# Mixture of experts behind windowed and latent attention: expert tiles from tables, weights copied per tile, rests of the groups in slots of 64 rows

## The chip, the core and the metric

The kernel runs on one core of one Trainium2 chip. The metric is the device time of one execution in microseconds, median of several runs. Everything is float32 unless said otherwise.

## What is computed

The input x has 4 sequences of 512 tokens with 128 features, 2048 tokens in all. The first part is attention (16 heads in windows of 32 keys and the 32 before them, and 8 heads over 64 pooled latents per sequence, both gated), a projection, the residual sum and a layer norm. The second part sends each token through two of eight experts:

```python
h = jnp.mod(x_flat[:, :TOP_K].sum(axis=1).astype(jnp.int32), E)
sel = jnp.stack([h, jnp.mod(h + 1, E)], axis=1)
def step(acc, params):
    e, W1e, b1e, W2e, b2e = params
    w = jnp.any(sel == e, axis=1).astype(x.dtype) / TOP_K
    y = jnp.maximum(x_flat @ W1e + b1e, 0.0) @ W2e + b2e
    return (acc + w[:, None] * y, None)
```

Then come the residual sum and a second layer norm. W1 is 128x512 and W2 is 512x128 per expert. Tokens with the same h form a group; group g goes through experts g and g+1 (mod 8). With the inputs of the runs the eight groups have 1052, 324, 132, 35, 10, 29, 131 and 335 tokens; among the first three sequences they have 772, 249, 101, 27, 10, 26, 102 and 249.

## The kernel before, in words

Each of the five engines has its own program; they meet at semaphores. The attention part goes over 16 tiles of 128 tokens (T = 16), in a loop that is written out (lines 1337 to 1407 on TensorE, with its counterparts on the other engines). It is a software pipeline: in step t TensorE does the scores of tile t, the weighing of tile t-1 and the projection of tile t-3, so there are three steps more than tiles. In the last of them `keep_busy` (line 1279) issues matmuls on a constant, so that TensorE has work.

Behind the first layer norm VectorE finds each token's group (`mark`, line 889), its row in a table in DRAM, `seg`, that has a stretch of rows per group (`place`, line 894), and GpSimd scatters the rows there by indirect DMA (`scatter`, line 507). A row is 128 features and the token's index.

The expert part works on tiles of 128 rows of `seg`, all of one group. One tile is: a turn of the rows (`columns`, line 1294), four matmuls up with W1 of the first expert (into bank bA), four with W1 of the second (banks bB and bC), relus with bias into `ha` and `hb`, and eight matmuls down with W2, four per expert, all summed in one bank. VectorE then adds the bias and the row itself, takes mean and variance (`moments`, line 1029), GpSimd makes the reciprocal deviation (`deviation`, line 554), VectorE finishes (`finish`, line 1043), and GpSimd stores the rows by indirect DMA, one store waiting for the last (`store`, line 561).

There are two kinds of tiles:

- FULL = 5 tiles are written out (lines 1416 to 1440 on TensorE). They hold full tiles of groups among the first three sequences, so they can start while the last sequence is still in attention. Which they are is computed on VectorE (`full_tiles`, `full_rows`, lines 920 and 933), loaded into registers by each engine, and their W1 comes by DMA into `w1f`. Their bias is picked by VectorE (`full_biases`, line 946).
- All others come in eight loops, one per group (lines 1441 to 1460), whose bounds are loaded from a table (`count_tiles`, line 956). Inside a loop the expert is known when the kernel is built, so weights and biases have fixed addresses and only the tile number k is in a register. Each group has at least one tile in its loop, the last with rows of padding. The weights of all experts lie in SBUF (`w1_s`, `w2_s`).

In a loop tile ScalarE does the four relus of `ha` and two of `hb`, VectorE the other two (BA = 2), and VectorE copies the turned rows.

`load_table` (line 304) waits for a semaphore and loads entries into a sequencer's registers. In the trace such a load is TENSOR_LOAD, FUSED_REGOPS and SEQ_ASSERT on the engine's queue, all at line 306. A loop's end is ALU_OP and COMPARE_BRANCH. [...]

With these inputs there are 5 tiles written out and 4+3+2+1+1+1+2+3 = 17 in the loops.

Of the kernel before, what the change touches and what calls it, by code (L numbers as in the profile page):

```python
# [13 lines left out]
P = 128  # L14
# [4 lines left out]
def bass_windowed_latent_attention_hash_moe(  # L19
# [29 lines left out]
    SLOTS = T + E + 1  # L49

    with ExitStack() as ctx:
# [84 lines left out]
        tile_table = sb("tile_table", [1, 2, E + 1], I32)  # L136
        full = sb("full", [P, 3, Z + E + 1])
        taken = sb("taken", [P, E])
        jrow = sb("jrow", [P, 2, FULL])
        jint = sb("jint", [P, 2, FULL], I32)  # L140
        reached = sb("reached", [P, FULL, E])
        cover = sb("cover", [P, FULL, E])
        gone = sb("gone", [P, FULL])
        chosen = sb("chosen", [P, FULL, E])
        b1d = sb("b1d", [P, 2, FC, E])
        b1p = sb("b1p", [P, FULL, 2 * FC, E])
        b1x = sb("b1x", [P, FULL, 2 * FC])
        full_table = sb("full_table", [1, 2, FULL], I32)
        tile_scale = sb("tile_scale", [P, E])
        found = sb("found", [P, 2, FULL])  # L150


        w1_s = sb("w1_s", [P, E, F])
        w2_s = sb("w2_s", [P, E, FC, D])
        b1r = sb("b1r", [E * FC, P])
        b1c = sb("b1c", [P, E * FC])
# [3 lines left out]
        fsum = sb("fsum", [P, HEAD, D])  # L160
        w1f = sb("w1f", [P, WR, 2, F])
        xs = sb("xs", [P, D])
# [9 lines left out]
        idx = sb("idx", [P, 1], U32)  # L172

# [11 lines left out]
        bA, bB, bX, bY, bC = bS[0][:, 0:512], bS[0][:, 512:1024], bS[1][:, 0:512], bV, bT  # L185

# [49 lines left out]
        b1d_ok = sem("b1d_ok")  # L236
        b1x_ok = sem("b1x_ok")
# [69 lines left out]

        def expand(eng, dst, src, mask, n):

            return eng.tensor_tensor(  # L310
                dst, src.unsqueeze(1).to_broadcast([src.shape[0], n, src.shape[1]]),
                mask.unsqueeze(2).to_broadcast([src.shape[0], n, src.shape[1]]), ALU.mult)

        @block.sync
        def _(sp):
# [19 lines left out]
            for t in range(T):  # L335
# [6 lines left out]
                if t >= T - E - 4:  # L342
                    e = t - (T - E - 4)
                    if e < E:
                        sp.dma_start(w1_s[:, e, :], W1[e]).then_inc(f_in, 16)
                        sp.dma_start(w2_s[:, e, :, :], W2[e].rearrange("(c p) d -> p c d", p=P)).then_inc(f_in, 16)
# [9 lines left out]
            for j in range(FULL):  # L356
                rows += load_table(sp, full_table[:, 1, :], [j], full_ok, E * SEG - P)
                if j == 0:
                    experts += load_table(sp, full_table[:, 0, :], [j], full_ok, E - 1)
# [3 lines left out]
                if 1 <= j + 1 < WR:  # L363
                    experts += load_table(sp, full_table[:, 0, :], [j + 1], full_ok, E - 1)
                    load_full_weights(j + 1)
            for j in range(WR, FULL):
                experts += load_table(sp, full_table[:, 0, :], [j], full_ok, E - 1)
                load_full_weights(j)

            tail = load_table(sp, tail_table, [0], tails_ok, E * SEG - P)  # L370
            first = [FULL] + load_table(sp, tile_table[:, 0, :], [1], table_ok, T + E, FULL)
            sp.sem_inc(tile_in, 16 * FULL)
            sp.sem_inc(kept, 16 * FULL)
            sp.wait_ge(scattered_late, 16 * KT_)

            for e in range(E):
                if e > 0:
                    tail += load_table(sp, tail_table, [e], tails_ok, E * SEG - P)
                    first += load_table(sp, tile_table[:, 0, :], [e + 1], table_ok, T + E, FULL)
                with sp.Fori(first[e], first[e + 1]) as k:  # L380
                    i = nc.s_assert_within(k - first[e], 0, T - 1,
# [1106 lines left out]
```

## Time and profile before

| | |
|---|---|
| time, median of 3 runs | 239.04 us (238.46 to 239.31) |
| the profiled execution | 238.23 us, span 236.5 us |
| busy: TensorE, its weight load, VectorE, ScalarE, GpSimd | 90%, 75%, 62%, 51%, 50% of the span |
| mean clock granted to TensorE | 0.986 of full speed |
| moved by DMA | 14.73 MB, 62 GB/s |

The span is the time from the first to the last instruction of the profiled execution. A float32 matmul is two records in the trace, each with a weight load of its own. A busy share is a mean over stages with different limits, so the table says only where to look; the rows below are read for single stretches.

### The profile page before, as it was taken

How to read it: one execution, taken by the hardware profiler on the slowest of the kernel's cores; microseconds unless marked ns; L12 is line 12 of the kernel's file. 1: busy time of each engine (PE TensorE's matmuls, PEld its weight loads, DVE VectorE, ACT ScalarE, POOL GpSimd, SP SyncE). 2: the span in 40 equal slices, each digit the busy share in tenths (PEclk: the TensorE clock that was granted, in tenths of full speed). 3: DMA queues.
4: the chain of work that ended last, by engine and by line, in shares of the span. 5: the costliest groups of instructions: out<-in, count | busy, mean ns of one | idle time of the engine just before them, and what ended most of it. 6: DMA issues, size and time to landing. Idle time of an engine off the chain costs nothing.

```text
span 236.5 us, 10737 instructions
## 1 busy us (share of the span) xinstructions
PE 212.2 (90%) x4009; PEld 176.2 (75%) x4009; DVE 147.3 (62%) x521; ACT 120.6 (51%) x360; POOL 117.8 (50%) x219
## 2 busy tenths in 40 slices
PE   6879999999998999998999988999999999999920
PEld 2445778767777667886776678989999999899920
DVE  6836448585877765888898616734655555555540
ACT  3546557765466646765656145754344434344400
POOL 6563034852544427762647601847646545455541
PEclk9999999999999999999999999999999999999995
DMA  4131120112232132130001365212121212121100
GB/s 100 58 94 47 49 96 3 45 52 91 91 78 66 47 103 72 43 96 15 28 25 36 117 201 151 96 38 76 40 62 44 56 43 57 27 48 36 35 22 7
DMA packets 18557, 14.73 MB, mean 62 GB/s; under 512 B 2647, under 2 KB 15547, under 8 KB 18513
## 3 DMA queue, kind: packets, MB, share of 16 engines
q1 hardware_dynamic: 17008, 11.83, 17.9%
q0 software_dynamic: 1216, 2.16, 2.8%
q8 instruction: 30, 0.49, 0.9%
q10 hardware_dynamic: 288, 0.13, 0.3%
q14 instruction: 15, 0.11, 0.2%
HBM read 11.43 MB, written 3.03 MB: 61 GB/s over the span
## 4 chain that ended last, share of the span: by engine, by line
PE 74%; DVE 6%; issue 5%; DMA 4%; POOL 3%; ACT 3%; SPq 1%; POOLq 0%; ACTq 0%; DVEq 0%
PE bS L1308 12%; PE bT L1251 7%; PE bV L1452 6%; PE bV L1459 5%; PE bS L1194 4%; PE bV L1266 4%; PE bS L1219 4%; PE bJ L1170 3%; PE bV L1323 3%; PE bT L1308 3%; PE bS L1233 2%; PE bL L1367 2%; PE bS L1201 2%; PE bV L1274 2%; DMA out<-yo,idx 2%
## 5 line engine op out<-in xcount | busy, mean ns | idle before, releaser
L680 ACT ACTIVATE ha<-bS,b1c 128x128 f32<-128x128 f32 x68 | 19.4, 368 | 38.0 <-PE bS L1308 38.0
L668 ACT COPY PTs<-bT 128x512 f32<-128x512 f32 (+3 forms) x48 | 25.9, 539 | 18.2 <-PE bT L1251 18.2
L567 POOL DMA_INDIRECT out<-yo,idx x18 | 19.4, 1076 | 17.5 <-POOL idx L563 9.6
L1251 PE MATMUL bT<-ident,Pr 128*128 128x128 f32 x168 | 27.2, 277 | 0.5 <-issue 0.4
L1308 PE MATMUL bS<-xsT,w_s 128*128 128x128 f32 x204 | 26.3, 279 | 1.1 <-issue 1.0
L1308 PEld LDWEIGHTS bS<-xsT,w_s 128*128 128x128 f32 x204 | 24.1, 192 | 2.2 <-issue 2.2
L498 POOL TENSOR_SCALAR rstd<-mv 128x1 f32<-128x1 f32 x16 | 3.8, 236 | 44.0 <-DVE mv L859 44.0
L1251 PEld LDWEIGHTS bT<-ident,Pr 128*128 128x128 f32 x168 | 19.5, 141 | 5.4 <-issue 4.1
L514 POOL DMA_INDIRECT groups<-x,pos x16 | 16.5, 1034 | 11.7 <-DVE pos L909 8.4
L655 ACT ACTIVATE Pr<-bS 128x512 f32<-128x512 f32 x32 | 20.1, 629 | 3.0 <-PE bS L1233 3.0
L814 DVE TENSOR_REDUCE mx<-bS 128x8 bf16<-128x512 f32 x32 | 21.4, 677 | 0.0
L819 DVE TENSOR_REDUCE mx<-bS 128x8 bf16<-128x128 f32 (+3 forms) x16 | 7.9, 491 | 20.6 <-issue 14.9
L1459 PE MATMUL bV<-w_s,hb 128*128 128x128 f32 x136 | 18.5, 277 | 0.0
L1452 PE MATMUL bV<-w_s,ha 128*128 128x128 f32 x136 | 18.1, 276 | 0.2 <-DVE ysum L1027 0.2
L1077 DVE TENSOR_SCALAR hb<-bT,b1c 128x128 f32<-128x128 f32 x34 | 10.5, 347 | 11.7 <-PE bT L1308 11.0
L1459 PEld LDWEIGHTS bV<-w_s,hb 128*128 128x128 f32 x136 | 16.7, 191 | 0.3
L1452 PEld LDWEIGHTS bV<-w_s,ha 128*128 128x128 f32 x136 | 16.5, 192 | 0.4 <-ACT ha L680 0.4
L1266 PE MATMUL bV<-Vx,PTs 128*32 128x18 f32 x1024 | 15.2, 186 | 1.3 <-DVE rem L835 0.8
L1266 PEld LDWEIGHTS bV<-Vx,PTs 128*32 128x32 f32 x1024 | 12.4, 111 | 4.5 <-issue 3.2
L631 ACT COPY Vx<-bJ 64x256 f32<-64x256 f32 x32 | 12.0, 374 | 7.0 <-PE bJ L1170 6.8
L504 POOL TENSOR_SCALAR x<-y,mv,rstd 128x128 f32<-128x128 f32 x15 | 13.0, 867 | 1.6
L559 POOL TENSOR_TENSOR rstd<-rstd,half 128x1 f32<-128x1 f32 x22 | 12.5, 567 | 1.7
(237 smaller groups left out, 496.9 us busy)
## 6 DMA issues: line engine op xcount, KB each, us to landing
w_s<-in_L_ffn_W SPq DMA_DIRECT2D x16, 256.0 KB
w1f<-in_L_ffn_W SPq DMA_DIRECT2D x10, 256.0 KB, 3.0
xrow<-groups SPq DMA_DIRECT2D x22, 64.5 KB, 1.9
xs<-groups SPq DMA_DIRECT2D x18, 64.0 KB
x_tok<-in_L_attn_x SPq DMA_DIRECT2D x4, 256.0 KB, 3.7
groups<-padrows SPq DMA_DIRECT2D x1, 516.0 KB, 6.0
b2r<-in_L_ffn_b SPq DMA_DIRECT2D x1, 512.0 KB, 3.4
out<-yo,idx POOLq DMA_INDIRECT x18
```

Source lines behind the costliest of these rows:

```text
L504: nc.gpsimd.tensor_scalar(x1[:, t, 0:D], y[:, q, :], mv[:, q, 0:1], rstd[:, q, :], ALU.subtract, ALU.mult).then_inc(ln_done, 1)
L514: nc.gpsimd.indirect_dma_start(seg, bass.IndirectOffsetOnAxis(ap=pos[:, t:t + 1], axis=0), x1[:, t, :], None).then_inc(done, 16)
L567: nc.gpsimd.indirect_dma_start(rows_out, bass.IndirectOffsetOnAxis(ap=idx[:], axis=0), yo[:, FULL - 1, :], None, bounds_check=T * P - 1, o ...
L655: nc.scalar.activation(Pr[:, t % 2, j, :].rearrange("p (z c) -> p z c", z=2), own[j], ACT.Exp, scale=SCALE).then_inc(exped[j], 1)
L668: nc.scalar.copy(PTs[:, j, 0:m, :], bT[:, 0:m * P].rearrange("p (c q) -> p c q", c=m)).then_inc(turned_out, 1)
L680: nc.scalar.activation(dst[:, c, :], src[:, c * P:(c + 1) * P], ACT.Relu, bias=bias_of(c)).then_inc(relu, 1)
L814: nc.vector.tensor_reduce(mx[:, j, :].rearrange("p (z h) -> p z h", z=2), own[j].rearrange("p z (h k) -> p z h k", h=4), AX.X, ALU.max).th ...
L1251: last = nc.tensor.transpose(bT[:, c * P:(c + 1) * P], Pr[:, t % 2, j, c * P:(c + 1) * P], ident[:])
L1266: last = mm(bV[i * W:(i + 1) * W, a * PW:(a + 1) * PW], PTs[:, j, c, i * W:(i + 1) * W], Vx[:, q, i, a, :], start=True, stop=True)
L1308: last = mm(bank_of(c)[:, c * P:(c + 1) * P], w[:, c * P:(c + 1) * P], xsT[:], start=True, stop=True)
L1452: mm(bY[:, 0:D], ha[:, c, :], w2_s[:, e, c, :], start=(c == 0), stop=False)
L1459: last = mm(bY[:, 0:D], hb[:, c, :], w2_s[:, a, c, :], start=False, stop=(c == FC - 1))
```

## The change

- FULL is 4, one tile fewer written out. The later entries of the same table, up to the number of full tiles among the first three sequences, are run by a first loop on all engines. A second loop runs the remaining tiles from a second table. Table 1 has 12 entries of row and expert, table 2 has 14; both are computed on VectorE, on one partition.
- In both loops each engine but GpSimd loads one entry per tile (`load_entry`). The expert is now in a register. ScalarE copies the two experts' W1 (128x512 each) into the fixed tiles `w1a` and `w1b`; W2 and the biases are addressed through the register. The weights have a ninth entry, a copy of expert 0, so that e+1 needs no modulo.
- BA = 1: in a loop tile ScalarE does five relus and VectorE three. The loops sum in bank bL instead of bV.
- A group's rest of at most 64 rows (a longer one takes a full tile) goes to a slot. Eight slots of 64 rows make four tiles. Eight passes, one per expert in the order 1, 2, 3, 0, 4, 5, 6, 7, take the two slots that use this expert: four matmuls up with 128 moving columns, four relus on ScalarE, and four matmuls down where both slots lie in the same tile, otherwise four pairs of matmuls with 64 stationary columns each. The four slot tiles have buffers and stores of their own.
- In the last attention steps 18 fillers of `keep_busy` go and four come, and the first upward passes, which stood between the last steps' matmuls, come behind the last projection. `rank_last` stands ahead of an upward pass instead of behind it. `full_biases` goes.

With the inputs of the runs there are 4 tiles written out, 4 in the first loop, 8 in the second, and the four slot tiles.

```diff
-    BA = FC // 2
+    BA = 1
-    FULL = (EARLY * P - E * (P - 1) + P - 1) // P
+    FULL = (EARLY * P - E * (P - 1) + P - 1) // P - 1
+    TS = P // 2
+    TT = E // 2
+    ORDER = [1, 2, 3, 0, 4, 5, 6, 7]
...
+        def load_entry(eng, tab, i, most):
+            return eng.value_load(tab[0:1, bass.ds(i, 1)], min_val=0, max_val=most)
...
@@ scalar
+            act.wait_ge(down, FULL)
+            nc.scalar.copy(fsum[:, HEAD, :], bY[:, 0:D]).then_inc(f_out, 1)
+            act.wait_ge(f_in, 32 * (E + 1))
+            def tile_of(e, k):
+                act.wait_ge(up_a, k)
+                nc.scalar.copy(w1a[:], w1v[:, bass.ds(e * F, F)]).then_inc(w1a_ok, 1)
+                act.wait_ge(up_b, k)
+                nc.scalar.copy(w1b[:], w1v[:, bass.ds(e * F + F, F)]).then_inc(w1b_ok, 1)
+                act.wait_ge(up_a, k + 1)
+                for c in range(FC):
+                    nc.scalar.activation(ha[:, c, :], bA[:, c * P:(c + 1) * P], ACT.Relu,
+                                         bias=bias_of(e)(c)).then_inc(relu, 1)
+                act.wait_ge(up_b, k + 1)
+                for c in range(BA):
+                    nc.scalar.activation(hb[:, c, :], bB[:, c * P:(c + 1) * P], ACT.Relu,
+                                         bias=bias_of(e + 1)(c)).then_inc(relu, 1)
+            f1 = load_bound1(act)
+            with act.Fori(FULL, f1) as k:
+                tile_of(load_entry(act, experts1, k, E - 1), k)
+            f2 = load_bound2(act)
+            with act.Fori(f1, f2) as k:
+                tile_of(load_entry(act, experts2, entry_of(k, f1), E - 1), k)
...
@@ vector
-            first = [HEAD]
-            for e in range(E):
-                first += load_table(dve, tile_table[:, 1, :], [e + 1], table_ok, T + E, HEAD)
-                with dve.Fori(first[e], first[e + 1]) as last:
+            with dve.Fori(HEAD, last1) as last:
+                tile_of(load_entry(dve, experts1, last + 1, E - 1), last)
...
+                    nc.vector.tensor_scalar(hb[:, c, :], bC[:, c * P:(c + 1) * P],
+                                            b1c[:, bass.ds(e * FC + FC + c, 1)], 0.0, ALU.add, ALU.max).then_inc(relu_b, 1)
...
@@ tensor
-                if t == T + 2:
-                    keep_busy(6)
-                    columns(0)
-                    keep_busy(4)
-                    up_full(0, 0)
-                    pe.wait_ge(f_in, 32 * E)
-                    experts = load_table(pe, full_table[:, 0, :], [0, 1], full_ok, E - 1)
-                if t > T:
-                    keep_busy(6 if t == T + 1 else 2)
                 if t >= 3:
                     pe.wait_ge(gated, t - 2)
                     nc.tensor.transpose(aT, att[:], ident[:]).then_inc(attT_up, 1)
+                if t == T + 2:
+                    columns(0)
+                    pe.wait_ge(f_in, 32 * (E + 1))
+                    experts = load_table(pe, experts1, [0, 1], full_ok, E - 1)
...
-            for e in range(E):
-                a = (e + 1) % E
-                with pe.Fori(first[e], first[e + 1]) as k:
-                    up(lambda c: bA, k, w1_s[:, e, :], up_a)
-                    up(lambda c: bB if c < BA else bC, k, w1_s[:, a, :], up_b)
-                    pe.wait_ge(biased, k)
+            def tile_of(e, k):
+                pe.wait_ge(w1a_ok, k + 1)
+                up(lambda c: bA, k, w1a, up_a)
+                pe.wait_ge(w1b_ok, k + 1)
+                up(lambda c: bB if c < BA else bC, k, w1b, up_b)
+                pe.wait_ge(loop_biased, k)
+                for c in range(FC):
+                    pe.wait_ge(relu, by_act + c + 1)
+                    mm(bL[:, 0:D], ha[:, c, :], w2f[:, bass.ds(e * F + c * P, P)], start=(c == 0), stop=False)
...
+            with pe.Fori(FULL, f1) as k:
+                tile_of(load_entry(pe, experts1, k, E - 1), k)
+            f2 = load_bound2(pe)
+            with pe.Fori(f1, f2) as k:
+                tile_of(load_entry(pe, experts2, entry_of(k, f1), E - 1), k)
...
+            for i in range(E):
+                slot_pass_up(i)
+                if i + 2 < TT:
+                    tail_turn(i + 2)
+                if i >= 1:
+                    slot_pass_down(i - 1)
+            slot_pass_down(E - 1)
```

`slot_pass_down` issues, for an expert whose two slots lie in different tiles:

```python
for q, g in enumerate(groups):
    r = (g % 2) * TS
    last = mm(slot_sum[g // 2][r:r + TS, 0:D], h[:, c, q * TS:(q + 1) * TS], w2_s[:, e, c, :],
              start=opens[q], stop=False, skip_group_check=True)
```

## Rows read from the trace of the kernel before

**Rows 1.** The page: busy us, share of the span, count.

```profile
PE 212.2 (90%) x4009; PEld 176.2 (75%) x4009; DVE 147.3 (62%) x521; ACT 120.6 (51%) x360; POOL 117.8 (50%) x219
```

**Rows 2.** Stretches: length, busy us (count) by engine, clock, DMA share, GB/s.

```profile
159.50:226.40 66.90, 65.46 (x563) 63.54 (x562) 37.98 (x137) 28.14 (x102) 37.05 (x72) 1.00 0.19 48
226.40:236.50 10.10, 0.00 (x0) 0.00 (x0) 1.48 (x5) 0.00 (x0) 3.15 (x5) 0.68 0.03 11
```

**Rows 3.** Chain in order of time, loops: start us, us, what.

```profile
206.74 0.40 issue
...
211.08 1.34 PE bS L1308 x12
212.42 0.45 PE bT L1308 x4
212.86 0.89 PE bV L1452 x8
213.76 0.11 PE bS L1303
...
214.76 0.26 issue
215.02 1.60 PE bS L1308 x12
```

**Rows 4.** Line 306, the table loads: ns min/median/max, first and last start.

```profile
L306 PEldq FUSED_REGOPS  x13: 151/151/165, 137.9 to 214.5; - x13
L306 PEldq SEQ_ASSERT  x13: 18/18/18, 138.2 to 214.8; - x13
...
L306 PEldq TENSOR_LOAD <-tile_table x8: 296/300/307, 151.1 to 214.2; - x8
...
L306 DVEq TENSOR_LOAD <-tile_table x8: 300/304/314, 161.1 to 216.2; - x8
```

**Rows 5.** Line 1445, the loop's branch on TensorE's sequencer.

```profile
L1445 PEldq COMPARE_BRANCH  x17: 67/208/251, 162.8 to 225.6; - x17
```

**Rows 6.** Timeline of VectorE in one loop tile.

```profile
212.99 0.61 DVE L1077 TENSOR_SCALAR hb<-bT,b1c 128x128 f32<-128x128 f32 x2 [0.47 <-PE bT L1308]
...
214.87 0.29 DVE L1027 TENSOR_TENSOR ysum<-bV,b2s 128x128 f32<-128x128 f32 x1 [0.42 <-PE bV L1459]
...
216.03 0.18 DVE L1037 BATCH_NORM_AGGREGATE mv<-st 128x2 f32<-128x6 f32 x1
```

**Rows 7.** Timeline of TensorE, 138 to 160 us.

```profile
138.91 0.39 PE L1281 MATMUL bJ<-spare 128*128 128x256 bf16 x2 [0.62 <-issue]
...
145.11 0.19 PE L1288 MATMUL bJ<-onehot,before 128*128 128x32 bf16 x1 [0.90 <-DVE onehot L885]
...
159.53 0.72 PE L1308 MATMUL bS<-xsT,w_s 128*128 128x128 f32 x5
```

**Rows 8.** Groups by form: busy us, mean ns, idle before.

```profile
L668 ACT COPY PTs<-bT 128x512 f32<-128x512 f32 x36 | 21.2, 590 | 18.0 <-PE bT L1251 18.0
...
L680 ACT ACTIVATE ha<-bS,b1c 128x128 f32<-128x128 f32 x68 | 19.4, 368 | 38.0 <-PE bS L1308 38.0
```

**Rows 9.** Timeline of VectorE, first and last of 13 table operations.

```profile
146.81 0.15 DVE L958 TENSOR_SCALAR tiles<-nextrow 1x8 f32<-1x8 f32 x1
...
149.28 0.26 DVE L970 CAST tile_table<-tiles 1x9 int32<-1x9 f32 x1
```

**Rows 10.** Chain in order of time, the last two stores.

```profile
226.91 2.31 DMA out<-yo,idx
...
230.59 1.05 POOL out L567
```

**Rows 11.** Timeline of TensorE, weighing with 32 stationary columns.

```profile
130.64 0.71 PE L1274 MATMUL bV<-GVx,PTs 128*32 128x72 f32 x32
```

**Rows 12.** Stretches of TensorE's clock; columns as in rows 2.

```profile
134.00:136.00 2.00, 1.46 (x12) 0.92 (x10) 0.51 (x3) 0.27 (x1) 1.61 (x3) 1.00 0.70 243
...
230.00:236.50 6.50, 0.00 (x0) 0.00 (x0) 0.00 (x0) 0.00 (x0) 1.05 (x1) 0.50 0.02 6
```

More of the change, by code:

```diff
@@ L390, in _, with load_tile @@
-            sp.wait_ge(xT_up, first[E])
+            def load_tile(k, row):
+                sp.wait_ge(kept, k * 16)
+                sp.wait_ge(xT_up, k)
+                sp.dma_start(xs[:], seg[bass.ds(row, P), 0:D]).then_inc(tile_in, 16)
+                sp.dma_start(xrow[:, bass.ds(k * XW, XW)], seg[bass.ds(row, P), :]).then_inc(kept, 16)
+            f1 = load_bound1(sp)
+            with sp.Fori(FULL, f1) as k:
+                load_tile(k, load_entry(sp, rows1, k, E * SEG - P))
+            f2 = load_bound2(sp)
@@ L727, in _ @@
                     nc.scalar.copy(fsum[:, j, :], bY[:, 0:D]).then_inc(f_out, 1)
[L728 removed]
+            relus(hb, bB, HEAD, up_b, bias_of(experts[HEAD] + 1), BA)
             columns_copy(FULL)
[L730 to L740 removed]
+            relus(hb, bB, HEAD, up_b, bias_of(experts[HEAD] + 1), FC, BA)
@@ new lines, in tile_of @@
+            def tile_of(e, last):
+                k = last + 1
+                dve.wait_ge(up_b, k + 1)
+                dve.wait_ge(down, k)
+                for c in range(BA, FC):
+                    nc.vector.tensor_scalar(hb[:, c, :], bC[:, c * P:(c + 1) * P],
+                                            b1c[:, bass.ds(e * FC + FC + c, 1)], 0.0, ALU.add, ALU.max).then_inc(relu_b, 1)
+                column_copy(k + 1)
+                dve.wait_ge(out_in, last * 16)
+                dve.wait_ge(rs_ok, k)
+                finish(FULL - 1)
+                dve.wait_ge(kept, k * 16 + 16)
+                dve.wait_ge(down, k + 1)
+                summed_up(bL[:, 0:D], b2f[:, bass.ds(e * D, D)], loop_biased)
+                moments(k, FULL - 1, xrow[:, bass.ds(k * XW, D)], loop_biased)
@@ new lines, in tile_of @@
+            def tile_of(e, k):
[4 more added lines that the diff above has]
+                pe.wait_ge(loop_biased, k)
+                by_act = k * (FC + BA) + FULL * (FC - BA)
+                for c in range(FC):
+                    pe.wait_ge(relu, by_act + c + 1)
+                    mm(bL[:, 0:D], ha[:, c, :], w2f[:, bass.ds(e * F + c * P, P)], start=(c == 0), stop=False)
+                columns(k + 1)
+                for c in range(FC):
+                    if c < BA:
+                        pe.wait_ge(relu, by_act + FC + c + 1)
+                    else:
+                        pe.wait_ge(relu_b, k * (FC - BA) + c - BA + 1)
+                    last = mm(bL[:, 0:D], hb[:, c, :], w2f[:, bass.ds(e * F + F + c * P, P)], start=False,
+                              stop=(c == FC - 1))
+                last.then_inc(down, 1)
@@ new lines, in slot_pass_up @@
+            def slot_pass_up(i):
+                e = ORDER[i]
+                pe.wait_ge(tail_out, max(e, E - 1 if e == 0 else 0) // 2 + 1)
+                if i >= 2:
+                    pe.wait_ge(slot_relu, FC * (i - 1))
+                cols = xTt[:, 0:E:E - 1, :] if e == 0 else xTt[:, e - 1:e + 1, :]
+                dst = bA if i % 2 == 0 else bB
+                for c in range(FC):
+                    last = mm(dst[:, c * P:(c + 1) * P].rearrange("p (g r) -> p g r", g=2),
+                              w1_s[:, e, c * P:(c + 1) * P], cols, start=True, stop=True)
+                last.then_inc(slot_up, 1)
```

457 lines of the change are left out of this document (277 added, 180 removed).

## The prediction

> **What bounds the kernel now.** I read the page's busy shares first: TensorE is busy 90% of the span, no other engine over 62% [rows 1]. Then the busy time by stretch [rows 2]. The loops over the experts' tiles run from 159.5 to 226.4 us, and in them TensorE is busy 65.5 of 66.9 us at the full clock; after its last matmul come 10.1 us in which it does nothing. Then the chain of waits in order of time [rows 3]: one tile in the loops is 12 + 4 matmul records upward, 8 downward, one turn of the next tile, 8 downward like the first, 1.34 + 0.45 + 0.89 + 0.11 + 0.89 = 3.68 us of TensorE without a gap. So the loops are bound by TensorE, and what matters is the number of tiles, and whatever makes TensorE wait between them. Three tiles have such a wait: they follow a group boundary where TensorE's own sequencer loads a table entry. There the engine is idle 0.26, 0.32 and 0.40 us and its first 12 records then take 1.60 instead of 1.34 us: 0.52 to 0.66 us lost, 4.20 to 4.34 us per tile [rows 3]. Boundaries without a load on TensorE's sequencer lose nothing.
>
> **The change, part by part.** The sum is made in the profiled execution (span 236.5, time 238.23 us); the median is 239.04, so 0.8 us is added at the end.
>
> Tiles. The inputs give groups of 1052, 324, 132, 35, 10, 29, 131 and 335 rows. Before, that is 22 tiles (5 written out, 17 in loops). After, a rest of at most 64 rows goes to a slot: 8+3+1+0+0+0+1+3 = 16 tiles, 4 written out and 12 in loops (4 in the first, 8 in the second). Six tiles at 3.68 us are 22.1 us less.
>
> Slots. Eight passes of 4 matmuls up (0.89 us, 8 records [rows 3]): 7.1 us. Down, the four odd experts need 4 matmuls each (0.89): 3.6 us. The four even ones need 4 pairs, each of two matmuls with 64 stationary columns and 128 moving ones. No row shows such a pair. From above it costs twice a full matmul, 1.79 us per pass; from below, the half that full overlap gives, 0.89. The nearest row has 32 stationary columns, four column groups in turn, 72 moving columns: 32 records in 0.71 us [rows 11], while at the rate of full matmuls (8 records of 128 columns in 0.89 us) they would take 2.0 us. They overlap, so I take 1.0 us per pass, 4.0 us. With four turns (0.4), the first turn and copy before anything can go up (0.7) and small gaps, 16.0 us; without overlap 19.2 us. ScalarE's part (32 relus of 0.37 us [rows 8], 11.8 us at most) lies beside it.
>
> Loop period. This decides. The two loops now load one entry per tile on TensorE, ScalarE, VectorE and SyncE. On TensorE's sequencer that is the load, 0.30 us, a register operation of 0.15 us and an assertion of 0.02 us [rows 4], some 0.65 us with the gaps between them. It can't run ahead: the sequencer issues the last downward matmul only when its relu is there, and behind it stand the branch, the load and then the next tile's first matmul. To the 4.20 to 4.34 us of a tile with a load [rows 3] come: the taken branch, 0.21 against 0.07 us when it falls through, and a register step behind it, which cost 0.2 us [rows 5]; the third relu of VectorE, 0.26 us later than its second, in exchange for one fewer on ScalarE (VectorE starts them as soon as the upward matmuls end [rows 6]), 0.1 us net; one wait for the copied weights and the address arithmetic of entry and weights, 0.1. Sum 4.6 us; from below 4.20 (only the load as before), from above 5.0.
> The other engines in that cycle: ScalarE has four relus and one relu, then the entry, then two copies of 128x512. A copy of this shape takes 0.59 us from PSUM [rows 8]; from SBUF no row shows it, I take the same, bounds 0.3 to 0.9. The first copy would be ready some 4.0 us after the tile's start, TensorE asks for it at 4.5; the second is asked for 0.89 us later. So the copies are hidden, by half a microsecond; without that cover each 0.1 us is paid 12 times. VectorE: its relus, turn copy, end of the previous tile, sum and moments finish 5.1 us after the tile's start (216.2 against 210.9 [rows 6]); with branch, entry load (0.30 us [rows 4], 0.7 with its register steps) and addresses it is back at 6.5, and is wanted at 4.6 + 2.1 = 6.7. It is nearly late too, so 4.6 can't shrink much below 4.4 by anything that helps TensorE alone. GpSimd's chain of one store behind another has a cycle of 3.68 us (226.91 to 230.59 [rows 10]) and no load in it: hidden.
> [...]
> The twelve tiles: 12 x 4.6 = 55.2, less 0.75 because the last has no successor, plus 0.6 for the bound that is loaded between the loops: 55.05 us from the first tile's start to the last downward matmul.
>
> Up to the loops. Before, the first loop tile starts at 159.53 [rows 7]. One tile fewer: -3.7. TensorE no longer idles for the last marks (0.90 us at 145.11 [rows 7]), as the last projection, which stood behind the first upward pass, two entry loads (0.62 us idle [rows 7]) and fillers, comes some 1.3 us earlier: -0.8. The first tile's upward passes now stand behind that projection and the loads: +0.6. That puts the end of the written-out tiles near 155.4. Then the new entrance: ScalarE must see the last downward matmul, copy its sum (128x128, 0.3), load the bound and an entry (1.3) and copy the weights (0.59) before TensorE has anything to do: +2.5, so the first loop tile starts at 157.9. VectorE: the table arithmetic grows from 13 operations in 2.7 us [rows 9] to some 24 in 4.5; it starts 1.3 us earlier, and VectorE is at the loop's first relus at about 159.7, when TensorE's upward part ends (157.9 + 1.8). Hidden, with nothing to spare: a VectorE that is 1 us late costs 1 us, once. SyncE's nine further loads and eight slot DMAs (0.33 us each) have a whole tile's time before TensorE asks for the slots: 0.
>
> End. From TensorE's last record (226.3) to the last store's start are 4.3 us (230.59 [rows 10]), then landing and the closing. After, the two last slot tiles go one behind the other through VectorE (1.35 us each), GpSimd (0.85) and two indirect stores (1.05 each [rows 6, 10]): 4.5 us. The drain stays 10.2 us.
>
> Sum: 157.9 + 55.05 + 16.0 + 10.2 = 239.1 us of span, 2.6 more than before; on the median 241.6 us.
>
> **Rivals.**
> Faster, by a cheap loop. If part of the entry load runs ahead, the period is the 4.1 us that the cheapest load tile would have without its slower restart; then 12 x 0.5 = 6 us come off: 235.6. The point of balance is a period of 4.38 us. For it: 22.1 us of removed matmuls are certain. Against it: the sequencer is held by the relus in each row that I could find. Chance 0.15.
> No change, period 4.3 to 4.45: 239.0. Chance 0.13.
> The pairs of 64 columns don't overlap: +3.2, 244.8. Against: rows 11. Chance 0.14.
> VectorE or ScalarE sets the period (5.0 us: dynamic addresses for each relu, or a slow copy from SBUF): +4.8, 246.4. Chance 0.12.
> The clock. Eighteen filler matmuls go and four come; twelve of those that go lay between 134.6 and 139. [...] After the change some 3 us there hold two short turns and nothing else. If the clock falls, two passes of 0.89 us go at half rate: +1.8, 243.4. Chance 0.06.
> The forecast (period 4.45 to 4.8) has 0.40.
>
> **How the numbers follow.** About 0.3% (0.7 us) can be told from no change. Faster: 0.15 and a little from the lower edge, 0.16. Same: 0.13 and what of the neighbours falls inside, 0.14. Slower: 0.70. The likeliest case gives 241.6, its own range 240 to 244. For 8 in 10 the range is cut below at a period of 4.25 (237.5), which leaves 0.09 out, and above at 246.5, the dear loop itself, which leaves 0.10.
>
> **What would show it.** In the changed kernel, TensorE's chain in the loops: a gap marked as issue ahead of each tile's first upward matmul, tile starts 4.6 us apart, the sequencer's load and branch inside that gap. ScalarE's weight copies ending before the gap does (if the gap ends with them, that is the dear-loop rival). Sixteen tiles; even and odd downward slot passes nearly alike. An idle stretch of some 2.5 us on TensorE between the written-out tiles and the loop. The drain after the last matmul still 10 us. It is wrong if tiles start under 4.4 us apart, if the entrance stall is missing, or if the slots take over 18 us.

## The result, and the profile after

The changed kernel takes 250.07 us (median of 4 runs, 248.74 to 250.99); the kernel before, beside it, 239.18 us (4 runs). The ratio is 1.0449, 95% interval 1.0385 to 1.0514: slower, as forecast, but by 10.9 us and not by 2.5, and outside the range of 237.5 to 246.5. A run over 1.5% above the fastest of its kernel is left out of the ratios, not of the medians, so a quotient of two medians can differ a little from the ratio beside them.

The page of the changed kernel, TensorE first; then the busy time by stretch (columns as in [rows 2]: length, busy us and count by engine, clock, DMA share, GB/s): the loops, the slots, the end, the stretch from 158.0 to 161.5 by itself, and the one behind it.

```profile
PE 209.5 (85%) x3965; PEld 171.1 (69%) x3966; DVE 143.9 (58%) x515; ACT 130.5 (53%) x370; POOL 113.9 (46%) x210
```

```profile
158.36:219.97 61.61, 51.09 (x397) 48.26 (x398) 28.52 (x104) 29.86 (x83) 25.01 (x49) 0.98 0.15 40
219.97:236.26 16.29, 16.05 (x163) 14.06 (x161) 4.11 (x15) 9.61 (x36) 6.05 (x11) 1.00 0.07 19
236.26:247.00 10.74, 1.10 (x10) 0.90 (x8) 2.61 (x10) 0.16 (x1) 4.22 (x7) 0.67 0.04 14
158.00:161.50 3.50, 3.14 (x15) 3.14 (x16) 0.22 (x1) 1.76 (x6) 2.27 (x4) 0.51 0.06 19
161.50:164.60 3.10, 2.26 (x20) 2.07 (x19) 1.80 (x7) 1.71 (x4) 0.97 (x3) 1.00 0.18 46
```

Before, the loops held TensorE busy 65.46 of 66.90 us [rows 2]; now they hold it busy 51.09 of 61.61. Fourteen microseconds of matmuls are gone from them and 10.5 us of idle time stand there. No engine is near full in that stretch: VectorE is busy 28.5 us, ScalarE 29.9. A stretch in which every engine has time left is bound by waits, or by something that the busy shares don't count.

The chain of waits in order of time (start us, us, what) shows one tile as [rows 3] did before.

```profile
204.98 0.88 issue
205.86 1.35 PE bS L1479 x10
207.21 0.67 PE bT L1479 x6
207.88 1.00 PE bL L1604 x8
208.88 0.11 PE bS L1474
208.99 1.03 PE bL L1611 x8
210.02 0.88 issue
210.90 1.35 PE bS L1479 x10
```

A tile takes 210.90 - 205.86 = 5.04 us, and the steps of the second loop lie between 5.02 and 5.09. Against the 3.68 us of a tile without a gap it has 0.88 us of issue ahead of the upward matmuls, 0.23 more in these (2.02 for 16 records, 1.34 + 0.45 before; [rows 3] had the same in a tile with a load, 1.60 for 1.34), and 0.25 more in the downward ones: 1.00 and 1.03 us for the 8 records that took 0.89. The first two were in the forecast, though smaller; the last wasn't. Why the upward records take 2.02 us is open: they take it also in the run below that has no gap ahead of them.

"Issue" is time in which the engine waits for nothing that the profile shows, so the next view is that of TensorE's sequencer by line (ns min/median/max, first and last start).

```profile
L342 PEldq TENSOR_LOAD <-table x12: 297/303/313, 156.5 to 215.1; - x12
L342 PEldq FUSED_REGOPS  x12: 151/151/161, 156.9 to 215.5; - x12
...
L1620 PEldq FUSED_REGOPS  x8: 78/78/82, 179.6 to 215.0; - x8
L1620 PEldq ALU_OP  x8: 32/32/32, 184.2 to 219.7; - x8
L1620 PEldq COMPARE_BRANCH  x8: 76/208/208, 184.3 to 219.8; - x8
...
L1611 PEldq FUSED_REGOPS  x48: 46/46/46, 162.4 to 219.5; - x48
```

Line 342 is the entry's load and line 1620 the second loop, with durations like those of [rows 4] and [rows 5]. The last row is new: 48 register operations for the 12 x 4 second downward matmuls, one for each matmul's address. The first four have the same.

The entrance to the loops:

```profile
156.20 0.28 ACTq L339
...
156.90 0.36 ACTq L342
...
157.69 0.63 ACT w1a L832
...
158.36 2.50 PE bS L1479 x10
160.86 1.00 PE bT L1479 x6
```

The timeline of TensorE has the same start, with the idle time before it and what ended that in brackets:

```profile
158.36 2.07 PE L1479 MATMUL bS<-xsT,w1a 128*128 128x128 f32 x8 [2.37 <-ACT w1a L832]
```

Bound, entry and copy of ScalarE stand one behind another, as forecast; TensorE's idle time there is 2.37 us. What I hadn't priced is behind it: the first tile's upward records take 2.50 + 1.00 us and not 1.35 + 0.67, because the granted clock is 0.51 of full speed from 158.0 to 161.5 and 1.00 before and behind it. That tile takes 6.3 us.

The slots, around the first pass with pairs of 64 columns:

```profile
223.76 0.89 PE bS L1638 x8
224.65 0.25 PE bS L1658
...
225.68 1.09 PE bS L1638 x8
```

The timeline shows the two matmuls of a pair side by side, one in each column group:

```profile
224.85 0.27 PE L1658 MATMUL bS<-w_s,hb 128*64 128x128 f32 x1
224.86 0.27 PE L1658 MATMUL bL<-w_s,hb 128*64 128x128 f32 x1
```

From the end of the matmuls up to the next ones up, 224.65 to 225.68, are 1.03 us for sixteen records of such pairs, against 0.89 for a pass of eight full ones. One behind the other they would take 1.79, so the pairs overlap. The slots take 16.3 us in all.

### The profile page after: what moved, and what is told of

It is laid out like the page before. It is cut to its first block, busy times and chain, and to the rows that moved or that the text cites. A ratio compares the mean times of both kernels' runs of the same rounds, so it can differ in the third digit from the quotient of the medians.

```text
span 247.0 us, 10859 instructions
## 1 busy us (share of the span) xinstructions
PE 209.5 (85%) x3965; PEld 171.1 (69%) x3966; DVE 143.9 (58%) x515; ACT 130.5 (53%) x370; POOL 113.9 (46%) x210
## 4 chain that ended last, share of the span: by engine, by line
PE 74%; issue 10%; DVE 5%; ACT 4%; DMA 2%; SPq 2%; POOL 1%; ACTq 1%; DVEq 0%; POOLq 0%
PE bS L1479 10%; PE bT L1422 7%; PE bL L1611 5%; PE bL L1604 4%; PE bS L1365 4%; PE bV L1437 4%; PE bS L1390 4%; PE bJ L1341 3%; PE bS L1638 3%; PE bT L1479 3%; PE bV L1494 3%; PE bS L1404 2%; PE bL L1531 2%; PE bV L1445 2%; PE bS L1372 2%
## 5 line engine op out<-in xcount | busy, mean ns | idle before, releaser
L623 POOL DMA_INDIRECT out<-yo,idx x13 | 13.8, 1059 | 27.7 <-DVE yo L1180 20.4
L1479 PE MATMUL bS<-xsT,w1a 128*128 128x128 f32 x96 | 14.5, 297 | 12.9 <-issue 9.0
L839 ACT ACTIVATE ha<-bS,b1c 128x128 f32<-128x128 f32 x48 | 13.7, 368 | 22.0 <-PE bS L1479 22.0
L1479 PEld LDWEIGHTS bS<-xsT,w1a 128*128 128x128 f32 x96 | 12.4, 202 | 14.9 <-issue 8.4
L1341 PE MATMUL bJ<-wvg,xT 128*32 128x64 f32 (+1 forms) x512 | 12.5, 228 | 2.3 <-issue 2.0
L1604 PE MATMUL bL<-w_s,ha 128*128 x96 | 13.9, 288 | 0.0
L1611 PE MATMUL bL<-w_s,hb 128*128 x96 | 13.9, 288 | 0.0
L359 POOL TENSOR_TENSOR Kx<-KT,slot 128x512 f32<-128x512 f32 x12 | 12.4, 1041 | 0.8 <-ACT KT L692 0.8
L1604 PEld LDWEIGHTS bL<-w_s,ha 128*128 128x128 f32 x96 | 12.8, 188 | 0.0
```

The costliest lines, as they stand in the source:

```text
L623: nc.gpsimd.indirect_dma_start(rows_out, bass.IndirectOffsetOnAxis(ap=idx[:], axis=0), yo[:, FULL - 1, :], None, bounds_check=T * P - 1, o ...
L839: nc.scalar.activation(ha[:, c, :], bA[:, c * P:(c + 1) * P], ACT.Relu, bias=bias_of(e)(c)).then_inc(relu, 1)
L1341: last = mm(bJ[r * W:(r + 1) * W, at:at + wide], xT[:, b % 2, w:w + W], wvg[:, c, 0:wide], start=True, stop=True)
L1479: last = mm(bank_of(c)[:, c * P:(c + 1) * P], w[:, c * P:(c + 1) * P], xsT[:], start=True, stop=True)
L1604: mm(bL[:, 0:D], ha[:, c, :], w2f[:, bass.ds(e * F + c * P, P)], start=(c == 0), stop=False)
L1611: last = mm(bL[:, 0:D], hb[:, c, :], w2f[:, bass.ds(e * F + F + c * P, P)], start=False, stop=(c == FC - 1))
```

## The experiments

They ran in four further measurements, and in each the kernel before was timed too: 246.69 us in the first (5 runs), 246.16, 246.60 and 247.43 us in the others. So whole times are compared by their ratios, and tiles by their period. That the loops of the kernel before are the same under both conditions is measured first.

**The kernel before, once more with a profile** (no edit).

> The kernel before, unaltered, for a profile of it under the conditions in which the experiments ran. Expected by every theory: the same time as the kernel before (ratio 1.0), its tile loops as long as in its first profile (66.9 us from the first upward matmul of the loops to the last downward one), and the 7 us by which it is slower there than in the first measurement all ahead of the loops, so that tile periods of the experiments may be compared across measurements and whole times by their ratios alone.

247.03 us, ratio 1.0007 (0.9968 to 1.0046). Timeline of TensorE (start us, us, engine line op; idle before and its releaser in brackets), the first matmuls of the loops and the last:

```profile
168.85 1.50 PE L1308 MATMUL bS<-xsT,w_s 128*128 128x128 f32 x12
...
234.12 1.06 PE L1459 MATMUL bV<-w_s,hb 128*128 128x128 f32 x8
```

From 168.85 to 235.2 are 66.3 us, 66.9 before. The loops hardly depend on the conditions; their start does, 168.85 against 159.53 [rows 7]. Part of that is TensorE's clock ahead of the loops: 0.54 from 135 to 140 us here, 1.00 in the first profile. The profiles below differ there too, so whole times of two versions that lie about 1% apart say little, and the conclusions rest on the loops.

**The changed kernel, once more** (no edit).

> The changed kernel unaltered, beside the next three on one chip. Every theory expects what was measured before: 1.04 to 1.05 times the kernel before, tiles of the loops 5.05 to 5.08 us apart, TensorE idle 2.4 us ahead of the first of them. It is there so that the others are compared with it under the same conditions.

259.08 us, ratio 1.0522 (1.0459 to 1.0584), a little above the first one's interval. Period 5.02 to 5.09 us in the second loop, as before.

**The load behind the upward matmuls.** My theory for the period: TensorE's sequencer pays for the entry's load behind the branch, where nothing can run ahead, and for a register address with each downward matmul. The rival: ScalarE's copies or VectorE set it.

```diff
                 up(lambda c: bB if c < BA else bC, k, w1b, up_b)
+                e = entry()
                 pe.wait_ge(loop_biased, k)
```

> TensorE's entry load stands after the two upward passes of a loop tile instead of ahead of them (the upward passes use the copied weights and need no entry). Theory A (TensorE's sequencer sets the period of 5.05 us, and 0.65 us of it are the load behind the branch): the load falls into the time in which the sequencer waits for the relus, the period drops by 0.65 to 0.75 us to some 4.35, 12 tiles give 8 to 9 us: 239.5 to 242 us of time. Rival B (ScalarE's weight copies or relus set the period): at most 1 us gained. Rival C (VectorE is just behind: it waits only 0.27 us for the upward matmuls): 0.27 x 12 = 3 us gained at most, and the wait of VectorE for TensorE gone.

250.24 us, ratio 1.0127 (1.0068 to 1.0186). The starts of two tiles:

```profile
189.34 1.13 PE L1479 MATMUL bS<-xsT,w1a 128*128 128x128 f32 x8
...
193.76 1.13 PE L1479 MATMUL bS<-xsT,w1a 128*128 128x128 f32 x8
```

The gap is gone and the period is 4.34 us (median of 11 steps, 4.25 to 4.42 but for the first and the one between the loops). The load itself is as long as before (303 ns median in both); it now runs while the engine works off sixteen upward matmuls. Its place cost 0.72 us a tile, 8.6 us in twelve. Both rivals, which allowed 1 us and 3 us in all, are out as the main cause. The time expected, 239.5 to 242 us, was for the first measurement; at the ratio of 1.0127 it would be 242.2 there.

**A second load per tile, not used.**

```diff
+                load_entry(pe, experts2, entry_of(k, f1), E - 1)
                 tile_of(load_entry(pe, experts2, entry_of(k, f1), E - 1), k)
```

> TensorE loads the entry twice per loop tile, one load behind the other, ahead of the upward passes. Theory A: 0.65 to 0.75 us more per tile, 8 to 9 us more in all, about 258.5 us. Rivals B and C: under 3 us more, as another engine's chain sets the period.

263.37 us, ratio 1.0673 (1.0611 to 1.0736).

```profile
207.12 1.13 PE L1479 MATMUL bS<-xsT,w1a 128*128 128x128 f32 x8 [1.53 <-issue]
```

Steps of 5.66 to 5.74 us in the second loop, 0.65 more for one more load, and the gap is 1.53 us for 0.88. Each load in this place is paid in full: the eleven steps take 64.8 us together, against 57.8 in the profile of the changed kernel once more. The whole time rose by less than the 8 to 9 us expected (ratio 1.0673 against 1.0522, some 4 us), as the loops also start 1.4 us earlier in this profile.

**Downward matmuls at constant addresses.** Left out: the right W2 for most tiles; expert 0's and 1's are always used.

```diff
-                    mm(bL[:, 0:D], ha[:, c, :], w2f[:, bass.ds(e * F + c * P, P)], start=(c == 0), stop=False)
+                    mm(bL[:, 0:D], ha[:, c, :], w2_s[:, 0, c, :], start=(c == 0), stop=False)
```

> The downward matmuls of the loop tiles read W2 of experts 0 and 1 at fixed addresses instead of through the register (their results belong to the wrong expert); loads and copies stay. Theory A in its second half (each downward matmul with a register address and a register wait costs the sequencer 0.22 to 0.26 us and leaves it no lead): 0.3 us less per tile, 3.6 us in all, between 1.5 and 6: about 246.5. If the register addresses are hidden: no change, within 0.7 us.

252.63 us, ratio 1.0238 (1.0166 to 1.031). The sequencer's rows of the second downward matmuls, and the next tile's start:

```profile
L1611 PEld LDWEIGHTS bL<-w_s,hb x96: 190/192/192, 171.4 to 223.3; 128*128 128x128 f32 x96
```

```profile
204.34 1.06 PE L1611 MATMUL bL<-w_s,hb 128*128 128x128 f32 x8
206.00 1.13 PE L1479 MATMUL bS<-xsT,w1a 128*128 128x128 f32 x8 [0.61 <-ACT w1a L832]
```

ScalarE's copy for that tile, and TensorE's load of the entry (line 342, 204 to 206.5 us):

```profile
204.82 0.62 ACT L832 COPY w1a<-w_s 128x512 f32 x1 [0.71 <-issue]
```

```profile
L342 PEldq TENSOR_LOAD <-table x1: 304/304/304, 205.2 to 205.2; - x1
...
L342 PEldq SEQ_ASSERT  x1: 18/18/18, 205.7 to 205.7; - x1
```

The register operations of line 1611 are gone, eight records take 0.89 us again, and the period is 4.55 to 4.63 us: 0.48 less, where 0.3 was expected. So the address cost 0.48 us a tile, where the forecast had 0.1 for it and a wait together. Half of it is in the downward matmuls themselves; the other half is in the gap behind them (0.61 us for 0.88), as the branch comes earlier: at 204.7, 0.7 us before the tile's last matmul ends, and not 0.4 us before it (204.6 and 204.98 in the changed kernel). The bracket names ScalarE's copy because it ends within the gap, but that is at 205.44, 0.56 us before the matmul starts. What fills the rest is TensorE's own load, which ends at 205.7, 0.3 us before the matmul, as in the changed kernel (205.6 and 205.86). So TensorE's sequencer still sets this period; in the changed kernel the copy was ready a microsecond ahead (204.81, matmul at 205.86).

**Copies of 32 columns instead of 512.** Left out: the other columns of W1 (zeros).

```diff
-                nc.scalar.copy(w1a[:], w1v[:, bass.ds(e * F, F)]).then_inc(w1a_ok, 1)
+                nc.scalar.copy(w1a[:, 0:32], w1v[:, bass.ds(e * F, 32)]).then_inc(w1a_ok, 1)
```

> ScalarE copies 32 instead of 512 columns of each W1 per loop tile (the upward matmuls then read zeros for the rest). Theory A: the copies end 1.0 us before TensorE asks for them, so only the first tile and the change of loops gain, 0.5 us each, together 0.5 to 1.5 us: about 249. Rival B: 0.4 us per tile, 5 us in all.

260.64 us, ratio 1.0563 (1.0497 to 1.0628).

```profile
L832 ACT COPY w1a<-w_s 128x32 f32 x12 | 2.6, 218 | 9.5 <-issue 9.5
```

```profile
207.90 1.13 PE L1481 MATMUL bS<-xsT,w1a 128*128 128x128 f32 x8 [0.91 <-issue]
```

A copy takes 0.22 us and not 0.62, and the period stays at 5.04 to 5.07 us with the same gap. The rival is out: the copies were hidden. The 0.5 to 1.5 us expected didn't show in the whole time; the loops start at 170.79 in this profile, against 165 to 167 in the three others of that measurement. The edit also sets both tiles to zero on VectorE ahead of the attention part (0.49 us each, at 2.5 and 3.1 us), and the granted clock is 0.72 between 10 and 20 us, 1.00 in the three others; whether the one led to the other is open.

**Both edits on TensorE at once.** Left out: the right W2, as above.

> Two edits at once on TensorE: the entry's register is loaded behind a tile's sixteen upward matmuls (as in the run where only that was done, which took the period from 5.06 to 4.34 us), and the downward matmuls read expert 0's matrix at constant addresses (alone: 5.06 to 4.58 us). Left out: the right W2 for most tiles. Theory A (both costs are TensorE's own sequencer and add up): the period is 4.34 minus 0.48 = 3.86 us, and the time falls a further 12 x 0.48 = 5.7 us below the late load alone, to a ratio near 0.99. Rival B (the engines beside TensorE set the next bound): copies of 2 x 0.62 us, four relus of ScalarE, and five operations of VectorE with a wait between each pair take 4.0 to 4.2 us a tile, and the period stays there; TensorE's idle time then stands as waits for ScalarE's copy or VectorE's relu and no longer as issue. Gain over the late load then 2 to 4 us.

247.41 and 254.50 us (2 runs, no interval; the profile is of the second, so only its loop is read, at clock 1.00 from 176 to 222 us). The steps of the second loop are 4.12 to 4.53 us, not 3.86: the two savings don't add up. VectorE's timeline shows what comes next:

```profile
212.96 0.18 DVE L1172 BATCH_NORM_AGGREGATE mv<-st 128x2 f32<-128x6 f32 x1
214.43 0.87 DVE L1211 TENSOR_SCALAR hb<-bT,b1c 128x128 f32<-128x128 f32 x3 [1.29 <-PE bT L1479]
```

TensorE's upward matmuls (211.66 plus 2.02) end at 213.7, and VectorE starts its relus 0.7 us later; before, it started 0.12 us behind them (212.99 in [rows 6], 212.87 in [rows 3]). The bracket names TensorE, but in those 1.29 us VectorE's own sequencer runs its branch, its load of the entry (0.30 us) and register operations. In a cycle of 4.24 us VectorE waits only 0.31 us, for TensorE's sum, and that sum needs VectorE's last relu. So VectorE's cycle, foreseen as "nearly late too", is the loop's next bound; this is read from the timeline, and no run relieves VectorE to test it.

**Fillers at the entrance**, on top of the late load.

```diff
             pe.wait_ge(summed, T)
+            pe.wait_ge(tails_ok, 1)
+            keep_busy(18)
             f1 = load_bound1(pe)
```

> The late load, and 18 filler matmuls between the written-out tiles and the first loop, from the moment at which the tables are out, while TensorE has nothing to do. Theory (the granted clock falls to half because TensorE idles 2.4 us at the entrance): the clock stays full, the first tile's upward half takes 1.35 us and not 2.5, and the time is 1.0 to 1.5 us below the late load alone, whose ratio to the kernel before was 1.013; so 1.006 to 1.009. Rival (the fall belongs to the loop's first tile, whatever stood ahead, or the fillers delay the bound's register load): no gain, or a loss of up to 1 us. If period and warm entrance are all, it is still no faster than the kernel before.

252.37 us, ratio 1.0244 (1.0193 to 1.0294). At their own place they do what they should:

```profile
166.82 2.13 PE L1452 MATMUL bJ<-spare 128*128 128x256 bf16 x18
169.34 1.16 PE L1479 MATMUL bS<-xsT,w1a 128*128 128x128 f32 x8 [0.40 <-ACT w1a L832]
```

The first tile's first eight records take 1.16 us, and from this tile's start to the next one's are 4.41 us; with the late load alone they took 2.07 and the tile 5.66. So 1.25 us are the clock's, and the fall does belong to the idle entrance: in the seven profiles of table loops without fillers the clock falls to 0.50 there, behind 1.99 us of idle time in the run with short copies and 2.35 to 2.38 in the others. But the next tile gives most of it back:

```profile
177.91 1.00 PE L1612 MATMUL bL<-w_s,hb 128*128 x6 [0.65 <-DVE hb L1211]
```

```profile
174.61 0.36 DVE L1180 TENSOR_SCALAR yo<-y,mv,rstd 128x128 f32<-128x128 f32 x1 [1.54 <-DMA out<-yo,xrow]
```

VectorE waits 1.54 us for the store of a written-out tile, comes late with its relus, and that tile takes 5.28 us instead of 4.37. From the first tile's start to the last one's are 49.2 us, 49.6 with the late load alone. So the whole time shows no gain, and it is above that of the late load (1.0244 to 1.0127). In this profile the clock fell once more, at 158.5, in 2.81 us of idle time within the written-out tiles (up to 158.98), before the first filler (166.82); the late load's profile has the same idle time (2.76 us) and no fall. Of ten profiles with such an idle time of 2.73 to 2.94 us three have the fall, two of them without fillers, so the fillers aren't its cause.

**No table at all: one guarded loop per group.** If running tiles by a table is what costs, loops with constant experts should be back at 3.7 us with the same slots.

```diff
-            f1 = load_bound1(pe)
-            with pe.Fori(FULL, f1) as k:
-                tile_of(load_entry(pe, experts1, k, E - 1), k)
...
+            for e in range(E):
+                if e + 1 > 4:
+                    first += load_first(pe, 0, FULL, [e + 1])
+                guarded(pe, first[e], first[e + 1], lambda k: tile_of(e, k))
```

> The changed kernel's slots of 64 rows stay; in place of its two table loops stand eight loops, one per group, each with its expert's addresses constant and each jumped over where its group has no tile left. So no register load per tile, no copies of weights by ScalarE, no register address in a matmul, but eight bounds and eight guards. Theory A (the loss is the price of running tiles by a table on TensorE's sequencer, the slots are sound): the period is 3.7 to 3.8 us, 12 tiles 45 us instead of 61.6, the guards and loop entries cost 0.3 to 0.6 us each (3 to 5 us in all), and with the slots' 16.3 and the drain's 10.7 us the time is 229 to 234 us against 239: ratio 0.96 to 0.98. Rival (entering a loop costs as much as the table's entry does, since each entry waits for a bound, a branch and cold buffers: 1.5 us and more each): 12 us more, ratio 1.0 or above. Rival C (the slots cost more than their own span shows, through the copies and the combining that follow them): ratio 1.0 or above with the loops' part short all the same, and a longer stretch from the last whole tile to the end.

254.72 us, ratio 1.0319 (1.0269 to 1.0368): better than the changed kernel beside it, slower than before. Within a group the period is 3.68 to 3.69 us (189.93, 193.61), as said. The loss is at the changes of group, and it begins on SyncE:

```profile
189.09 0.12 PE bS L1449
...
196.65 2.65 DMA xs<-groups
...
199.35 0.33 PE bS L1449
...
200.59 2.71 issue
```

SyncE may load the next tile's rows only when TensorE has turned the last ones (189.09); then it passes groups without a tile, two reads from the table each, and its transfer starts at 196.65. TensorE is idle 2.9 us for it, then 2.7 us for its own bounds and guards, and its clock is 0.50 from 200.5 to 207.3 us. The eight slot loads, behind the last group, cost up to 1.1 us more at a turn.

**Rows ahead.** SyncE loads each tile's rows once, without that wait, and each slot behind its group; VectorE copies the rows that TensorE turns.

```diff
-                sp.wait_ge(xT_up, k)
-                sp.dma_start(xs[:], seg[bass.ds(row, P), 0:D]).then_inc(tile_in, 16)
...
+                dve.wait_ge(kept, k * 16 + 16)
+                nc.vector.tensor_copy(xs[:], v).then_inc(xs_ok, 1)
```

> The guarded loops again (one per group, constant experts, slots of 64 rows unchanged), with SyncE's queue taken off the path: a tile's rows are loaded once, into their lasting place, with no wait for TensorE; VectorE copies the next tile's rows into the small buffer that TensorE turns (0.3 us a tile, behind the tile's moments); a group's bound is read ahead of its guard and its row inside it; and each group's slot is loaded behind that group's loop and not all eight behind the last. Theory (the guarded run lost 9 to 12 us to SyncE: 2.9 us at 199, 2.7 us behind it and the half clock after that, 2.3 us around the last turn and the slots' first turns): the waits for transfers of rows go, the twelve tiles take 12 x 3.75 + 2 us, the span is about 239 us where the kernel before takes 246 in a call like the last, and the ratio is 0.97 to 0.98. Rival (VectorE, which gets a fifth operation and a wait for a transfer in each tile, becomes the bound at 4.0 us or more, or the copy comes too late for the turn): period 4.0 to 4.3, 3 to 6 us more, ratio 0.985 to 1.0. Rival (the guards and the bounds' loads of TensorE, ScalarE and VectorE cost 1 us and more a group in themselves): TensorE's idle time stands as issue at each change of group, ratio about 1.0.

251.59 us, ratio 1.0162 (1.0104 to 1.0221). The waits for rows are gone; the issue gap isn't, and the half clock comes with it as in the run before (0.50 from 205.4 to 212.2 us; the profile is of a run of 253.81 us):

```profile
202.66 1.01 PE bL L1601 x6
203.67 2.98 issue
206.64 2.50 PE bS L1464 x10
```

**TensorE's bounds read earlier**, four of them where it waits for a written-out tile's sum.

```diff
+                if j == 2:
+                    first += load_first(pe, 0, FULL, [1, 2, 3, 4])
                 down_full(j, 0)
```

> The guarded loops with rows loaded ahead, and all of TensorE's bounds read earlier: four where it waits for the sum of a written-out tile (2.9 us idle at 158.7 in the last run), three within the last two written-out tiles, one inside the second group; none at a change of group any more. Theory (the 2.98 us of issue at 203.7 in the last run are three lazy reads of bounds, 0.30 + 0.21 + 0.08 us each, beside three branches of 0.21 to 0.33 us, and the half clock behind it follows from the idle time): the idle time at that change falls to 0.9 us or less, the clock stays full there (another 2.5 us), the 0.55 us ahead of the first tile goes too; 5 to 6 us in all, and a ratio of 0.99 to 1.0 to the kernel before. Rival (ScalarE and VectorE read the same bounds at the same change, 0.7 us a group, and become what TensorE waits for): 1 to 2 us less gained, ratio 1.0 to 1.005. Either way the guarded form would hardly beat the kernel before.

250.42 us, ratio 1.0119 (1.0052 to 1.0186).

```profile
200.46 1.00 PE L1601 MATMUL bL<-w_s,hb 128*128 128x128 f32 x6 [0.54 <-DVE hb L1185]
202.47 1.38 PE L1464 MATMUL bS<-xsT,w_s 128*128 128x128 f32 x10 [1.00 <-issue]
...
207.04 1.00 PE L1601 MATMUL bL<-w_s,hb 128*128 128x128 f32 x6 [1.30 <-DVE hb L1185]
```

```profile
173.50 0.36 DVE L1154 TENSOR_SCALAR yo<-y,mv,rstd 128x128 f32<-128x128 f32 x1 [3.20 <-DMA out<-yo,xrow]
```

The gap shrinks from 2.98 to 1.00 us (0.66 for each of the three loads) and the clock stays full (1.00 from 196 to 208 us), as expected; but the rival holds too: VectorE's relus, late from its own reads of the bounds, stop TensorE for 0.54 and 1.30 us there. A third loss was in no theory: in the second tile TensorE waits 1.48 us for VectorE's sum, and VectorE had waited 3.20 us for the store of a written-out tile to land. Twelve tiles now take 53.4 us (166.12 to 219.56) and the slots 16 more, where the kernel before takes 66.3 for all. Together that is some 3 us more, most of what the tile fewer ahead of the loops saves. None of these versions beats the kernel before.

## Why the prediction was wrong

Its direction held, and so did its sum but for one line and the clock behind the entrance. Point by point, in the profiled execution:

| term | forecast | measured |
|---|---|---|
| start of the loops | 157.9 | 158.36 |
| twelve tiles | 55.05 | 61.61 |
| slots | 16.0 | 16.29 |
| end | 10.2 | 10.74 |
| span | 239.1 | 247.0 |

**The step that failed** is "one wait for the copied weights and the address arithmetic of entry and weights, 0.1" within the loop period of 4.6 us. The period is 5.07. The experiment with constant addresses puts the downward addresses alone at 0.48 us a tile, and that is the miss of 0.47. (The terms as written give 4.60 to 4.74, as they start from 4.20 to 4.34; I took the lower end.) I had counted address arithmetic as some operations per tile; it is one register operation before each of eight downward matmuls, 46 ns, beside a 32 ns step for the relu's wait. TensorE's engine needs 0.22 us for such a matmul's two records (0.89 / 4), and with the register it takes 0.25 to 0.26 (1.00 and 1.03 / 4). My reading is that the sequencer has no lead left, ends later, and everything behind the branch starts later; shown is what the constant addresses give back. Eleven steps times 0.47 are 5.2 us; the clock at the entrance is 1.2, the last tile 0.2: 6.6 us.

**The load in the gap** was read rightly: "it can't run ahead", and its place costs 0.72 us by the late load (0.65 by the second load), where [rows 4] gave 0.65 with its gaps. The trace of the kernel before shows the sequencer beside the relus: TensorE's takes its steps for the third and fourth downward matmul at 212.68 and 212.94 us, 0.05 us behind the ends of ScalarE's second and third relu (212.63 and 212.89), which the matmuls ahead of these need, and behind the last of ScalarE's relus (213.66) come the branch at 214.05 and the load at 214.18. Yet I took its cost from the tiles of before that have a load, 0.52 to 0.66 us with the slower restart, plus branch. That hid the size of the repair: one line, moved behind two others, gives back 0.72 us a tile, and the rival "part of the entry load runs ahead" needs that edit; the changed kernel as it stands shows none of it.

**The copies** are hidden by a microsecond (0.5 forecast) and take 0.62 us (0.59 taken over from a copy out of PSUM); short ones don't change the period. **VectorE** was rightly called nearly late: it was forecast at its relus 6.5 us after a tile's start and wanted at 6.7; in the changed kernel it starts them at 208.14, 0.26 us behind the last upward matmul (207.88), and it seems to be what stops the loop at 4.2 us when TensorE is relieved. **GpSimd**'s stores were hidden in the changed kernel (VectorE never waits for one in the loops), but not once TensorE is faster: 1.54 us of wait with the fillers, 3.20 in the last version.

**The clock** was looked for in the wrong place. The rival expected a fall at 134.6 to 139, where fillers go; the changed kernel has none there: clock 1.00 from 134 to 140, although TensorE is idle 1.38 and 1.29 us in it. The rival's half rate is in [rows 12]: 0.50 from 230.0 on, 3.6 us behind TensorE's last matmul (226.4 [rows 2]). The forecast itself had 2.5 us of idle time at the entrance (2.37 measured). I priced the idle time and put what follows it at nothing, without a reason; it was 1.2 us.

**Pairs of 64 columns** overlap, 1.03 us against 1.0; that rival is out. **The rest** came as forecast: four tiles written out and twelve in loops, 0.6 us more between the loops (5.67 for 5.07), the stall for the last marks gone. The start of the loops was met a little better than the text has it: 159.53 - 3.7 - 0.8 + 0.6 is 155.6 and not 155.4, so the terms give 158.1; 158.36 came.

The range ended at a period of 5.0, a bound "from above" for which no row stood. The 5.07 us that came, with 1.2 us of clock and 1.3 us by which the median lies above the profiled run, went through it.

## What to carry to other kernels

Where a loop runs short pieces by a table, count the instructions of the busiest engine's sequencer per piece, one for each matmul that has a register in its address (46 ns each here), and compare their time with what the engine needs; busy shares don't show them. Put a register load behind work that the engine can run off, not behind the loop's branch; here that is worth 0.72 us a tile. Look when the engine that a bracket names was done before you believe it: here a copy that had ended 0.56 us earlier stood as the cause. And where an entrance leaves the engine idle for two or three microseconds, price the slower clock behind it too: here 1.2 us behind 2.37 us of idle time.

## What the runs showed that I had not expected

- A register address costs TensorE's sequencer 46 ns for each matmul, and eight records with it take 1.00 to 1.03 us instead of 0.89; constant addresses gave back 0.48 us per tile of eight such matmuls.
- A halved clock lasted 3.4 us behind 2.4 us of idle time (clock 0.51 from 158.0 to 161.5), and there was none behind 0.40 us after fillers. Behind 2.73 to 2.94 us of idle time inside the written-out tiles it fell in three profiles of ten.
- Passing a group without a tile isn't free: on TensorE's sequencer a bound (0.30 us load, 0.15, 0.02) and a taken branch of 0.21 to 0.33 us, 2.98 us of gap for three bounds (rows ahead); 1.00 us is left without the loads.
- Two matmuls with 64 stationary columns in different column groups run together: 0.11 us from pair of records to pair of records in both.
